# A two-half mixer kernel: the last state, its product and the last pass by token halves, layer norm at the borders on VectorE, late weights, and another order of VectorE's work in the linear half

## The reference

```
x = x + linear_attention(layernorm(x))     # 16 heads of 16, phi = softplus + 1e-6, running sums over tokens
x = x + ffn(layernorm(x))
x = x + softmax_attention(layernorm(x))    # 16 heads of 16, causal, ALiBi bias, biases on q, k, v, o
x = x + ffn(layernorm(x))                  # the same weights as the first ffn
```

```
f, i = sigmoid(x Wf + c Uf + bf), sigmoid(x Wi + c Ui + bi);  g = tanh(x Wc + c Uc + bc);  c = f*c + i*g
```

## Time and profile before

| | us |
|---|---|
| median of 3 runs | 2843.21 (2839.76 to 2859.43) |
| profiled execution, its time | 2839.7 |
| its span, first to last instruction | 2837.9 |
| PE busy | 2249.2 |
| DVE busy | 1674.6 |
| ACT busy | 1261.3 |
| POOL busy | 828.1 |

### The profile page before, as it was taken

One profiled execution on the slowest core, in us unless ns is written; L12 is line 12 of the kernel. 1 busy time (PEld: TensorE's weight loads), 2 busy tenths in 40 slices (PEclk: granted clock), 3 DMA queues, 4 the chain that ended last, 5 costly groups with the idle time before them and its releaser, 6 DMA issues.

```text
span 2837.9 us, 57192 instructions
## 1 busy us (share of the span) xinstructions
PE 2249.2 (79%) x24094; PEld 1195.2 (42%) x24195; DVE 1674.6 (59%) x3769; ACT 1261.3 (44%) x2023; POOL 828.1 (29%) x692
## 2 busy tenths in 40 slices
PE   1568888878888777239889999999999999999952
PEld 0346555555555544103234344443444434433331
DVE  4446465564744533237767676676777767676216
ACT  1314334243333222005556665666656656665613
POOL 1432331333411101432324243242532413212110
PEclk9789999999999987658999999999999999999976
DMA  3001010110100101221222122121231211213052
GB/s 95 30 16 46 16 61 16 46 38 24 46 16 31 46 11 57 74 86 50 95 65 71 59 91 87 56 74 62 76 102 61 72 39 62 70 35 106 21 188 118
DMA packets 127439, 171.33 MB, mean 60 GB/s; under 512 B 8864, under 2 KB 94880, under 8 KB 127184
## 3 DMA queue, kind: packets, MB, share of 16 engines
q1 hardware_dynamic: 123088, 167.15, 17.9%
q10 hardware_dynamic: 4096, 0.53, 0.1%
HBM read 91.11 MB, written 76.02 MB: 59 GB/s over the span
## 4 chain that ended last, share of the span: by engine, by line
PE 58%; DVE 16%; issue 9%; ACT 6%; DMA 4%; POOL 3%; ACTq 3%; SPq 2%; POOLq 0%; DVEq 0%
PE general L864 9%; PE out_of_heads L755 8%; PE general L549 8%; PE scores L696 6%; PE scores L672 4%; DVE maxima L1348 3%; PE general L875 3%; PE general L535 3%; PE turned_scores L710 3%; ACTq L1068 3%; PE general L516 3%; PE out_of_heads L628 2%; DMA k_stacks<-k_stack 2%; PE scores L586 2%; PE out_of_heads L638 2%
## 5 line engine op out<-in xcount | busy, mean ns | idle before, releaser
L1348 DVE TENSOR_REDUCE maxima<-scores 128x1 f32<-128x512 f32 (+3 forms) x1536 | 796.7, 552 | 363.7 <-PE scores L672 232.7
L1047 ACT ACTIVATE probs_turned<-turned_scores 128x512 f32<-128x512 f32 x1152 | 682.7, 600 | 521.9 <-PE turned_scores L672 271.5
L696 PE MATMUL scores<-k_stacks,q_stacks 51*128 51x512 bf16 (+3 forms) x1536 | 451.3, 338 | 55.7 <-DVE maxima L1348 49.5
L710 PE MATMUL turned_scores<-q_stacks,k_stacks 53*128 53x512 bf16 (+3 forms) x1536 | 441.7, 331 | 40.5 <-ACT probs_turned L1047 40.4
L696 PEld LDWEIGHTS scores<-k_stacks,q_stacks 51*128 51x128 bf16 x1536 | 125.5, 95 | 302.3 <-DVE maxima L1348 204.7
L672 PE MATMUL scores<-mask_scores,identity 64*128 64x256 bf16 (+3 forms) x954 | 249.1, 261 | 0.0
L672 PE MATMUL turned_scores<-mask_turned,identity 64*128 64x128 bf16 (+3 forms) x969 | 247.6, 256 | 0.0
L1589 POOL TENSOR_SCALAR ln<-x_for_attention,ln_mean_var,ln_rstd 128x256 f32<-128x256 f32 x128 | 159.0, 1255 | 256.8 <-DVEq L1475 133.4
L1527 POOL TENSOR_TENSOR state_low<-state_doubled,state_high 128x2048 bf16<-128x2048 f32 x16 | 65.1, 4071 | 520.3 <-ACT state_high L995 520.3
L1610 POOL TENSOR_TENSOR ln_low<-ln 128x512 bf16<-128x512 f32 x128 | 134.4, 1060 | 203.8 <-DVE ln L1330 203.8
L864 PE MATMUL general<-ln_turned_high,w_high 64*128 64x512 bf16 (+1 forms) x597 | 127.9, 381 | 73.9 <-ACT qk_block L1079 55.1
(11 more groups left out here) (225 smaller groups left out, 5233.8 us busy)
## 6 DMA issues: line engine op xcount, KB each, us to landing
x_after_attention<-x_residual SPq DMA_DIRECT2D x16, 1024.0 KB, 5.2
x_times_wo<-x_wo_out SPq DMA_DIRECT2D x64, 256.0 KB, 2.2
k_stacks<-k_stack SPq DMA_DIRECT2D x64, 212.0 KB
q_stacks<-q_stack SPq DMA_DIRECT2D x64, 204.0 KB
x_for_attention<-in_x SPq DMA_DIRECT2D x8, 1024.0 KB, 5.5
x_residual<-in_x SPq DMA_DIRECT2D x8, 1024.0 KB, 5.5
x_for_attention<-x_after_attention SPq DMA_DIRECT2D x8, 1024.0 KB, 12.6
ffn_h<-x_times_wo SPq DMA_DIRECT2D x32, 256.0 KB, 6.8
```

The lines of the kernel that those rows point to most:

```text
L696: mx = pe.matmul(bank_s[:, first * P:(first + tiles) * P], QS[at:at + QROWS, r, i * P:(i + 1) * P], KS[at:at + QROWS, r, k0 * P:(k0 + tile ...
L710: ex = pe.matmul(bank_t[:, first * P:(first + tiles) * P], KS[at:at + KROWS, r, j * P:(j + 1) * P], QS[at:at + KROWS, r, i0 * P:(i0 + tile ...
L1047: nc.scalar.activation(PR[:, s % SLOTS, :], TB[s % 2][:, :], ACT.Exp).then_inc(sem["ex_taken"], 1)
L1348: r = dve.tensor_reduce(MP[:, gg % 2, g, at:at + 1], max_bank[m][:, first * P:(first + tiles) * P], AX.X, ALU.max)
```

## The change

- **Last state by halves.** In stage 8 of both phases, tokens 0 to 511 are cast (ACT, at k = 105) and their low is made (now on DVE, k = 106) as soon as gate group 1 is done; PE multiplies them with Uo at k = 115, between gate units 7 and 8, and DVE takes them at k = 117 or 118. The second half follows after the last gates. POOL has no part in the last state.
- **Last pass.** A piece is now half the tokens (rows 0 to 511 or 512 to 1023), not half of each partition's rows. Eight pieces need the first state half only; sums, tanhs and adds of the first four stand inside stage 8's slots, the rest of the first eight around `last_state_low`.
- **h of batch 0, chunks 0 and 1** gets its tanh on ACT inside phase 1's stage 8 (k = 129 and 131).
- **Layer norm on DVE** also for the first norm of batches 0 and 1 of phase 1, batch 0 of phase 2, and the second norm of batch 7 of phase 2 (`by_vector`). In phase 1, batch 1's statistics move from k = 62 to 76 to k = 6 to 20 of stage -1, and its normalise to k = 21; POOL's lows for it stand before `split_q`.
- **Late weights.** x of batch 0 is the first DMA. Weights q, k, v, o are split on DVE after batch 0's norm; the eight ffn weights in stage -1 after all else, with two own stages in the unused `ON`, and the state is set behind them. PE waits for each round where it is first used.
- **Order.** Phase 1's gates move one place later, to j = 16, so behind `take_chunk`; DVE's normalise from k = 43 to 46 to 45, 47, 48, 50.
- **SP.** In stage -1 of phase 2, `load_h` 2 and 3 of batch 1 stand before `load_group(0)`, and `load_group(1)` behind `store_qk` 2 and 3.
- **Statistics of phase 2's first norm** wait for `h_added` by pairs of tiles, not for all four.

```diff
+def by_vector(phase, which, b):
+    if phase == 1:
+        return which == 2 or b < 2
+    return (which, b) in ((1, 0), (2, B - 1))
...
+        WS = [flat(ON[:, 4 * n:4 * n + 4, :]) for n in range(2)]
...
+            load_x(0)
             sp.dma_start(COL[:, :], cols).then_inc(sem["const_in"], 16)
...
-            load_weights(0, 2, 2)
-            load_x(0)
-            load_weights(8, 4, 0)
-            sp.wait_ge(sem["w_split"], w.next("w_split", 2))
-            sp.wait_ge(sem["const_ready"], w.next("const_ready"))
+            for r in range(2):
+                load_weights(0, r, QK[:, r, :], r)
+            for r in range(2):
+                load_weights(8, r, WS[r], 2 + r)
+            sp.wait_ge(sem["const_ready"], 1)
...
+                if b == -1:
+                    for r in (2, 3):
+                        sp.wait_ge(sem["w_split"], r + 1)
+                        load_weights(8, r, WS[r % 2], 2 + r % 2)
...
-                return t[b].rearrange("(p n) d -> p (n d)", p=P)[:, half * KT * CH:(half + 1) * KT * CH]
+                return t[b][half * CH:(half + 1) * CH].rearrange("(p n) d -> p (n d)", p=P)
...
-                if b == -1:
-                    load_group(0)
-                    load_group(1)
                 if batch_in(b + 2):
                     load_h(b + 2, 2)
                     load_h(b + 2, 3)
+                if b == -1:
+                    load_group(0)
...
                     store_qk(b + 1, 2)
                     store_qk(b + 1, 3)
+                if b == -1:
+                    load_group(1)
... PE
+                if s == B * BATCH + HALF_DONE + 11:
+                    state_part(0, lambda c: general_for("dve", "cu"), False)
+            state_part(1, lambda c: general_for("dve", "cu"), False)
...
+                if s == B * BATCH + HALF_DONE + 11:
+                    state_part(0, bank_of_state, True)
+            state_part(1, bank_of_state, True)
... ACT
+            def last_state_high(half):
+                if half:
+                    act.wait_ge(sem["gate_used"], w.next("gate_used"))
+                else:
+                    act.wait_ge(sem["gate_used"], w.seen["gate_used"] + 1)
+                at = slice(half * CH, (half + 1) * CH)
+                nc.scalar.copy(CP[0][:, :, at], CS[:, :, at]).then_inc(sem["state_high"], 1)
...
+                if s == B * BATCH + HALF_DONE + 1:
+                    last_state_high(0)
+                if s == B * BATCH + HALF_DONE + 18:
+                    final_tanh(0, 2)
+                if s == B * BATCH + HALF_DONE + 25:
+                    final_tanh(2, 4)
+            last_state_high(1)
+            final_tanh(4, 2 * B)
... DVE
+            def last_state_low(phase, half):
+                dve.wait_ge(sem["state_high"], (phase - 1) * (B + 1) + B + half)
+                at = slice(half * CH, (half + 1) * CH)
+                dve.tensor_tensor(CP[1][:, :, at], CS[:, :, at], CP[0][:, :, at], ALU.subtract
+                                  ).then_inc(sem["state_split"], 1)
...
-                    if 43 <= k < 47:
-                        if k == 43:
+                    if k in (45, 47, 48, 50):
+                        if k == 45:
                             dve.wait_ge(sem["xt_dve"], turned_before(1, "ln2", pb))
-                        normalise(k - 43)
+                        normalise(1, XR, (45, 47, 48, 50).index(k))
...
-                    if k in (87, 105, 123, 141):
-                        gates(1, (k - 87) // 18)
+                    if k in (88, 106, 124, 142):
+                        gates(1, (k - 88) // 18)
                 if batch_in(fb):
+                    at = k + 56 if fb == 1 else k
...
+                    if by_vector(1, 1, fb) and at == 77:
+                        if turned_before(1, "ln1", fb):
+                            dve.wait_ge(sem["xt_dve"], turned_before(1, "ln1", fb))
+                        for c in range(4):
+                            normalise(0, XA, c)
+                if b == -2 and k == 80:
+                    split_weights(0, 0, [QK[:, r, :] for r in range(2)], 0)
+                if b == -1 and k == 80:
+                    split_weights(8, 4, [WS[r % 2] for r in range(4)], 2)
+                    set_state()
...
+                if s == B * BATCH + HALF_DONE + 2:
+                    last_state_low(2, 0)
+                if s == B * BATCH + HALF_DONE + 14:
+                    state_part(0)
+                    final_sum(0)
+                    final_sum(1)
+                if s == B * BATCH + HALF_DONE + 24:
+                    final_sum(2)
+                    final_sum(3)
+                    final_add(0)
+                    final_add(1)
+            for n in range(4, B):
+                final_sum(n)
+                if n == 4:
+                    last_state_low(2, 1)
+                final_add(n - 2)
+            state_part(1)
+            for n in range(B, 2 * B + 2):
                 if n < 2 * B:
...
```

More of the change, by code:

```diff
@@ L54 @@
 HALF_ROWS = 64
+HALF_DONE = 104
 TAIL = 9
@@ L288, in _, with load_weights @@
             w = Counts()
[L290 to L297, removed]
+            def load_weights(first, r, stage, done):
+                for m in range(2):
+                    src = weights[first + 2 * r + m].rearrange("(k p) e -> p k e", p=P)
+                    dst = stage[:, m * KT * D:(m + 1) * KT * D].rearrange("p (k e) -> p k e", k=KT)
+                    sp.dma_start(dst, src).then_inc(sem[f"w_in{done}"], 16)
             def store_block(par, r, part_of, done):
@@ L954, in turns @@
                     turn_both(XN, XL, k // 2 - 28)
-            pe.wait_ge(sem["w_split"], w.next("w_split", 2))
+            pe.wait_ge(sem["w_split"], 8)
             for s in STAGES:
@@ L1020, in raw_in @@
                 n = 4 * nb + r
+                if c == 0 and n < 2:
+                    act.wait_ge(sem["w_split"], n + 1)
                 if c == 0 and n >= 2:
@@ L1155, in _, with final_tanh @@
                 fill(1, s // BATCH, s % BATCH)
+                if s == B * BATCH + HALF_DONE + 1:
+                    last_state_high(0)
+                if s in (B * BATCH + HALF_DONE + 25, B * BATCH + HALF_DONE + 27):
+                    tanh_h(0, (s - B * BATCH - HALF_DONE - 25) // 2)
+            last_state_high(1)
+            def final_tanh(first, last):
+                for n in range(first, last):
+                    act.wait_ge(sem["fin_sum"], n + 1)
+                    a = FW[n % B][n // B]
+                    nc.scalar.activation(a, a, ACT.Tanh).then_inc(sem["fin_tanh"], 1)
             for s in STAGES:
@@ L1253, in _, with split_weights @@
             dve.wait_ge(sem["const_ready"], w.next("const_ready"))
-            def split_weights(first, rounds, slot):
-                for r in range(rounds):
-                    dve.wait_ge(sem[f"w_in{r % 2}"], w.next(f"w_in{r % 2}", 32))
+            def split_weights(first, slot, stages, done):
+                for r, stage in enumerate(stages):
+                    at = f"w_in{done + r % 2}"
+                    dve.wait_ge(sem[at], w.next(at, 32))
                     for m in range(2):
                         s = slot + 2 * r + m
-                        stage = QK[:, r % 2, m * KT * D:(m + 1) * KT * D]
+                        part = stage[:, m * KT * D:(m + 1) * KT * D]
                         scale = 0.5 if s in HALF else HD ** -0.5 if first == 4 and s == Q_ else None
                         if scale is not None:
-                            step(dve.tensor_scalar(stage, stage, scale, None, ALU.mult))
-                    stage = QK[:, r % 2, :]
+                            step(dve.tensor_scalar(part, part, scale, None, ALU.mult))
                     s = slot + 2 * r
@@ L1427, in fill_softmax @@
                             dve.sem_inc(sem["stat1_2"], 1)
+                    if k == 77 and by_vector(2, 1, fb):
+                        dve.wait_ge(sem["xt_dve"], turned_before(2, "ln1", fb))
+                        for c in range(4):
+                            normalise(0, XA, c, 2)
+                if b == B and k == 41:
+                    dve.wait_ge(sem["xt_dve"], turned_before(2, "ln2", pb))
+                    for c in range(4):
+                        normalise(1, XR, c, 2)
             def fill(b, k):
@@ L1594, in layer_norm @@
                 done = 4 * (norms_to(phase, f"ln{which}", b) - 1)
-                if (phase, which) != (1, 2):
+                if not by_vector(phase, which, b):
                     pool.wait_ge(sem[f"stat{which}_{phase}"], b + 1)
```

148 lines of the change are left out of this document (76 added, 72 removed).

## The result

The changed kernel took **2733.48 us** (median of 4 runs, 2728.38 to 2735.02), beside 2846.8 of the kernel before on the same chip: a ratio of 0.9586, with a 95% interval of 0.9564 to 0.9609. That is within the range and 34 us above the forecast of 2699. The profiled execution took 2732.81 us, its span 2730.7, so 107.2 us less than the span before, where the terms had summed to 144.

The account below looks back on a forecast made before the run. PE, busy 79%, was taken to bound the kernel, with gains only in its idle places: 25 + 44 + 15 + 37 + 23 = 144 off 2839.7 gives 2696, as a median 2699 us; range 2672 to 2742 (8 in 10).

Parts of the forecast that it names:

- Start, 25: Kernel start: x first, norms on DVE and later weights bring batch 1's first turned half 25 us earlier (15 to 33).
- Linear half, 44: Phase 1 stages: taking the chunk before the gates removes PE waits at gate groups and stage turns, 44 us (20 to 55).
- 6 x 2.25 = 13.5: Stage turns of the linear half: six 3.45 us waits fall to 1.2, gaining 13.5 us.
- Border, first part, 15: Between phases: state by halves, h's chunks 0 and 1 done ahead, norm on DVE; 15 us (9 to 19).
- Border, second part, 37: Between phases: h's loads issued before group loads; first maxima 41 us earlier, group 1 4 late: 37 us (15 to 41).
- rival B: Border: group loads stay the bound, the second border term falls to 15, total 2721 us; chance 0.11.
- End, 22.7: Kernel end: last norm on DVE 7.9, early products -3.6, shorter work after last gates 18.4; 22.7 us (14 to 25).
- A (masks): Linear half: masks set `chunk_out`, so the 1.55 us waits only move; 32 us less gain, 2731 us; chance 0.12.
- C: Start gives only 10 us, as batch 1's norm delays phi fully and `split_q` waits on POOL: 2714 us; chance 0.07.
- E: Linear half: chunk turned later than the tanh, so `take_chunk` ahead of gates delays them: slower, 2921 us; chance 0.01.
- F: Everywhere touched: other chains set each place, so no effect, 2843 us; chance 0.02.
- D: Stage starts and borders: less idle keeps the granted clock up, 20 us more gain, 2679 us; chance 0.07.

Follow-up runs that it names:

- the second trace: The changed kernel run once more, unaltered, for another trace: 2731.93 us, 0.9577 of the kernel before.
- the late cast: Changed kernel with ACT's state cast moved behind the next stage's two turned halves, and GpSimd's state low behind the chunks' low: 2720.82 us.
- the low part: On top of the kernel with the cast moved later, GpSimd's low of a batch's last chunks held until the fourth gate operations are done: 2700.02 us.
- norms_pool: Changed kernel with both layer norms of the softmax half's borders back on GpSimd: 2740.1 us, 0.9601 of the kernel before.

## Why the prediction was right, and where it was not

**Start, 25: right.** 24.2 in the first trace at the point that the prediction named, 24.9 in the second, and 24.4 at the second's first gates. The 2 us for x ahead of the constants and the 5 for batch 1's norm amid DVE's work hold together; neither was tried apart, and no run took the start's edits back: this term is read from landmarks alone.

**Linear half, 44: failed in one step.** Inside a stage the lead rises by 5.1 us over three gate groups (40.5 us from first to fourth gates before, 35.4 after), seven times 5.1 = 36, where I had 32.5 for 21 waits. The failing step is "6 x 2.25 = 13.5" at the stage turns. The wait fell by just that, but nothing came of it: on average the lead falls by 0.3 us over a turn. I named what follows the chunk on PE and on DVE but not what stands behind the gates on ACT: the cast, and behind it the turned halves that PE wants next. The sum allowed 2 us "for what reappears as smaller waits"; it was 9.7 for ACT's turned half and 4.1 once for GpSimd's low part, together 13.8. The runs with the late cast and the low part show that the turn did hold this and more: 695.5 us for the half instead of 750.5 before, 55 gained.

**Border, first part, 15: right.** 55.0 to 69.4 is 14.4. The norm's share is 7.7 by norms_pool, for 7.9; the products between the gate units cost 2.9 to 3.8 by the lead, for 2.6.

**Border, second part, 37: failed.** From 69.4 the lead went to 103.9 for group 0 and to 91.2 in batch 2, 22 us. The step that failed is the time of a group load: 19 to 20 us at the window's rate. That rate was read from 6 us in which the load ran at 46 GB/s. The trace of the kernel before shows about half that rate later in the same load:

```profile
1213.00:1218.00 5.00, 0.00 (x0) 0.00 (x0) 0.00 (x0) 0.00 (x0) 0.00 (x0) 0.50 0.07 25
```

Group 0's semaphore got its last count at 1218.7 there, 25.2 us after the issue, with no load of h or store of x behind it yet. In the changed kernel it got it at 1149.6, after 24.5. So the load did not slow; it was sized 5 to 6 us too short, and that is most of why the lead rose by 34.5 and not by 41. Group 1 then took some 33 us from its issue to its maxima, beside the stores and x, and the issue itself came 28.8 us behind group 0's where the prediction had 15.5, since SP stood in the issues before it. The bound of 15 was rival B, and the measured 22 lies nearer to it than to the forecast. The rule of the Trainium skill that I had beside the sum ("DMA: Bandwidth & Descriptors", Why a DMA increments its semaphore by 16 and not by 1) made this term 35, since I put only the stores behind on the slow engine. Its use was not as a correction of the sum but as a remedy: 31 us by cutting the rows.

**End, 22.7: right in the sum, in part by luck.** +6.3 at the norm (7.9 said), -3.2 (said -3.6), +18.8 (said 18.4), together 21.9. The norm itself is worth 3.5: the kernel with it back on GpSimd also gains 2.7 us over the kernel before at this place, and no run says from what. The rest of this term is read from landmarks alone.

The rest, 5.9 us lost between batch 2 and the last norm and 4.4 in the first stages, had no step. For the 4.4 the second trace shows that it is scatter of the clock; the 5.9 are of the size of that scatter. 24.2 - 4.4 + 35.2 + 14.4 + 21.8 - 5.9 + 21.9 = 107.2.

**Rivals.** A (masks) did not happen: the wait for `probs_turned` is 38.3 us in seven before and after. B came in part: group 0 did not slow, group 1 did. C, E and F did not. D did not in the changed kernel (mean clock 0.922 before, 0.923 after), and the clock rose only when the stage turns were closed, to 0.934 with the low part behind the gates.

## What to carry to other kernels

When a wait of one engine is shortened, go on along that engine to the next thing it needs and read the queue of whoever makes it: here the gain of six waits lay behind a 1.9 us cast that nobody was in a hurry for. When a load's window shows a low DMA share and SP's issues stretch to several us, look at the number of rows before reordering the queue: 51 and 53 rows cut at 48 gave 31 us, the whole new order 18.5. A load's rate over a few us is not its rate over the whole: follow it to its landing. A difference of 4 to 6 us between landmarks of two single traces is to be seen in a second trace before it is explained.

## What was not expected of the hardware

- A VectorE operation with two SBUF inputs (128x512, 0.69 us) took 2.38 us beside a GpSimd operation of 1.90 us that started 0.4 us earlier, which itself took 2.27; in total 11.9 us in seven places.
- Eight DMAs instead of four for a group of 0.83 MB cut its time to the first use from 25.2 to 11.1 us, and the issue of the 1 MB store behind it from 8.72 to 0.38 us: behind the uncut loads SP's own issues grew long.
- The same chunk of 106 matmuls took 8.21 or 9.55 us at a granted clock of 1.00 or 0.82; over 21 head groups of the softmax half the traces differ by up to 9 us, at 0.99 and 0.98.
